# Reordering the row gathers of a fused graph-attention and routed-FFN kernel: the optional gathers and their waits

## What is computed

```python
xp = (x @ W).reshape(n, H, C)
alpha = leaky_relu(a_src[src] + a_dst[dst], 0.2)
w = exp(alpha - amax[dst]) / denom[dst]
agg = segment_sum(xp[src] * w[..., None], dst)
x = x + elu(agg.reshape(n, H * C) + bias)
weights = einsum('bsd,do->bso', layernorm(x), wr) + br      # top half is selected
y = gelu(sel @ w1 + b1) @ w2 + b2;  processed = y * w_sel
x = x + (processed + layernorm(x))
```

## Time and profile before

| | |
|---|---|
| timed runs, median of 3 | 2207.0 us |
| profiled execution: span, first to last instruction | 2573.5 us |
| profiled execution: its own time beside the span | not given |
| PE busy, share of the span | 1981.2 us, 77% |
| DVE busy | 1581.4 us, 61% |
| GpSimd busy | 1554.5 us, 60% |
| ACT busy | 744.5 us, 29% |
| mean granted TensorE clock | 0.870 of full |
| DMA | 369.12 MB, 143 GB/s |

### The profile page before, as it was taken

The page is one execution under the profiler, slowest core; times in us unless marked ns, Lnnn a source line. Parts: engine busy times, 40 slices in busy tenths (PEclk is TensorE's granted clock), DMA queues, the critical chain, the costliest instruction groups (busy, mean ns, idle before and its releaser), DMA issues.

```text
span 2573.5 us, 29095 instructions
## 1 busy us (share of the span) xinstructions
PE 1981.2 (77%) x9511; PEld 1633.8 (63%) x9512; DVE 1581.4 (61%) x3510; ACT 744.5 (29%) x1478; POOL 1554.5 (60%) x1626
## 2 busy tenths in 40 slices
PE   8935877877877877878778877877777777877787
PEld 6723666666666666666666666666666666666666
DVE  4555655665655655656656665666665665666576
ACT  4512222222322222322232232232232232223223
POOL 2366666666666666666666666666666666666630
PEclk9967988888888889889888888988988988889889
DMA  8844444444444444444444444444444444444447
GB/s 287 276 143 121 123 134 124 132 138 120 137 138 118 132 135 124 135 140 120 134 137 128 130 136 124 134 134 130 128 134 131 127 139 124 131 136 136 119 159 312
DMA packets 157137, 369.12 MB, mean 143 GB/s; under 512 B 46646, under 2 KB 73682, under 8 KB 155699
## 3 DMA queue, kind: packets, MB, share of 16 engines
q0 software_dynamic: 75088, 208.19, 30.1%
q1 hardware_dynamic: 74706, 145.62, 16.9%
q10 hardware_dynamic: 7184, 13.41, 1.4%
HBM read 328.20 MB, written 38.89 MB: 143 GB/s over the span
## 4 chain that ended last, share of the span: by engine, by line
POOL 38%; issue 23%; PE 19%; another core or an unknown queue 9%; DVE 3%; DMA 3%; ACT 2%; POOLq 1%; DVEq 0%; SPq 0%; ACTq 0%
POOL rows L692 38%; PE ag_ps L1057 7%; PE h_ps L1021 4%; PE ag_ps L934 3%; PE y_ps L1040 3%; DMA rows<-node_rows,ends 3%; POOLq L402 1%; DVE oh L1366 1%; DVE rows L1404 1%; ACT hT L808 1%; PE ag_ps L1128 0%; ACT L808 0%; PE ag_ps L1129 0%; ACT L812 0%
## 5 line engine op out<-in xcount | busy, mean ns | idle before, releaser
L692 POOL DMA_INDIRECT rows<-node_rows,ends x1563 | 1512.9, 968 | 850.6 <-issue 482.5
L1057 PE MATMUL ag_ps<-rows,oh 128*128 128x260 f32 x3518 | 845.9, 401 | 47.5 <-DVE rows L1404 34.8
L1021 PE MATMUL h_ps<-xnT,w1s 128*128 128x256 f32 x1568 | 534.0, 500 | 419.2 <-DVE zz L1385 227.1
L1057 PEld LDWEIGHTS ag_ps<-rows,oh 128*128 128x128 f32 x3518 | 716.7, 204 | 180.3 <-DVE rows L1404 37.8
L1021 PEld LDWEIGHTS h_ps<-xnT,w1s 128*128 128x128 f32 x1568 | 377.0, 250 | 517.9 <-DVE zz L1385 234.8
L1404 DVE TENSOR_TENSOR rows<-rows,xl_ps 128x512 f32<-128x512 f32 (+3 forms) x392 | 503.1, 1346 | 47.2 <-issue 26.5
L1385 DVE TENSOR_TENSOR zz<-rows,edge_dm 128x72 f32<-128x72 f32 x98 | 22.9, 233 | 695.0 <-DMA rows<-node_rows,ends 656.4
L1040 PE MATMUL y_ps<-w2s,hT 128*128 128x256 f32 x1568 | 368.0, 386 | 12.2 <-DVE oh L1366 9.2
L831 ACT COPY rows<-rows 128x780 f32<-128x780 f32 x97 | 81.6, 842 | 998.6 <-DMA rows<-node_rows,ends 998.6
L1040 PEld LDWEIGHTS y_ps<-w2s,hT 128*128 128x128 f32 x1568 | 301.7, 194 | 66.7 <-DVE oh L1366 16.6
L1366 DVE TENSOR_TENSOR oh<-xl_ps,dloc 128x2304 f32<-128x2304 f32 x98 | 249.0, 2541 | 0.0
(11 more groups left out here) (243 smaller groups left out, 1433.7 us busy)
## 6 DMA issues: line engine op xcount, KB each, us to landing
dbc<-dst SPq DMA_DIRECT2D x97, 576.0 KB
rows<-node_rows,ends POOLq DMA_INDIRECT x1563
selfr<-node_rows SPq DMA_DIRECT2D x98, 130.0 KB
base<-in_x SPq DMA_DIRECT2D x14, 896.0 KB, 7.1
base<-in_x SPq DMA_DIRECT2D x49, 256.0 KB
ffn_rows<-yb ACTq DMA_DIRECT2D x48, 256.0 KB
node_rows<-base SPq DMA_DIRECT2D x13, 910.0 KB, 5.7
base<-in_x_turned SPq DMA_DIRECT2D x14, 384.0 KB, 7.7
```

The source lines that it names most:

```text
L692: pool.indirect_dma_start(out=rows[:, b, t, :], out_offset=None, in_=table, in_offset=bass.IndirectOffsetOnAxis(ap=ends[:, b, t, 0:1], axi ...
L1021: last = nc.tensor.matmul(h_ps[:, m * PAIR:(m + 1) * PAIR], w1s[:, c, n * P:(n + 1) * P], xnT[:, c, :], start=(c == 0), stop=(c == DC - 1))
L1057: product = nc.tensor.matmul(ag_ps[b][:, 0:ROW], oh[:, b, t, :], rows[:, b, t, :], start=(t == 0), stop=False)
```

## The change

The optional gathers of a block (from the third block on) move from the end of its required ones to behind the sixth (`OPTIONAL = 5`, tile 8), with the wait for the carry, the load of the number and the two `If`s. The wait for the second layer moves to ahead of the block's first required gather, as `y_ok >= w - 5`, and the last block has it too. In the written-out form the waits for `y_ok`, `ld_ends`, `lk_ok`, `freed` and `carry_ok` are no longer made by `wait_apart` but by `pool.wait_ge` directly ahead of the gather (`held`). `optional_landed` and the table loads that stand for places of extra tiles become `value_load` with bounds.

```diff
@@ -64,7 +64,7 @@
     LOW_BITS = 8
     DIGITS, LOW_DIGITS = (32 - LOW_BITS) // 2, LOW_BITS // 2
     FREED = 6
-    LOOKED_UP, SUMMED, SECOND_LAYER = 4, (8, 11, 13), TILES - 2
+    LOOKED_UP, SUMMED, OPTIONAL = 4, (8, 11, 13), 5
     COLS = 8
     FAR = 2.0 ** 20
 
@@ -402,9 +402,12 @@
             return nc.s_assert_within(eng.value_load(win[0:1, bass.ds(COLS * w + k, 1)]), 0, most,
                                       skip_runtime_bounds_check_because="the window table holds counts and places of the edges' tiles, which lie within their number")
 
+        def counted_before(eng, w, k):
+
+            return eng.value_load(win[0:1, bass.ds(COLS * w + k, 1)], min_val=0, max_val=NW * EP // P)
+
         def optional_landed(eng, w):
-            landed = eng.value_load(win[0:1, bass.ds(COLS * w + 7, 1)])
-            return nc.s_assert_within(landed, 16, 16 * (NW + 3), skip_runtime_bounds_check_because="a parity's first node block has one gather or more, each later one two at most")
+            return eng.value_load(win[0:1, bass.ds(COLS * w + 7, 1)], min_val=16, max_val=16 * (NW + 3))
 
         def all_extra(eng):
 
@@ -418,7 +421,7 @@
             with eng.If(extras > 0):
                 n = entry(eng, w, 1, EP // P)
                 with eng.If(n > 0):
-                    before = entry(eng, w, 2, NW * EP // P)
+                    before = counted_before(eng, w, 2)
                     with eng.Fori(0, n) as j:
                         body(j, before + j)
 
@@ -431,7 +434,7 @@
             with eng.If(flag > 0):
                 with eng.Fori(0, NW) as w:
                     n = entry(eng, w, 3, EP // P)
-                    before = entry(eng, w, 4, NW * EP // P)
+                    before = counted_before(eng, w, 4)
                     with eng.If(n > 0):
                         with eng.Fori(0, n) as j:
                             body(w, j, before + j)
@@ -674,55 +677,62 @@
                 gather_row(k, m_row, m_go)
 
 
+            def held(w, semaphore, value):
+
+                if isinstance(w, int):
+                    pool.wait_ge(semaphore, value)
+                else:
+                    wait_apart(pool, (semaphore, value))
+
             def follow(w, started):
 
                 if started == LOOKED_UP:
-                    wait_apart(pool, (lk_ok, w + 1))
+                    held(w, lk_ok, w + 1)
                 for k in range(GROUPS):
                     if started == SUMMED[k]:
-                        wait_apart(pool, (freed[k], w))
-                if started == SECOND_LAYER and known(w, 5) and not (isinstance(w, int) and w == NW - 1):
-                    wait_apart(pool, (y_ok, w - 4))
+                        held(w, freed[k], w)
 
             def window(w, i, b):
-                if not known(w, 2):
-                    pool.wait_ge(ld_ends[b], 16 * (i + 1))
-
                 def gather(t, arrived):
                     pool.indirect_dma_start(out=rows[:, b, t, :], out_offset=None, in_=table,
                                             in_offset=bass.IndirectOffsetOnAxis(ap=ends[:, b, t, 0:1], axis=0)).then_inc(arrived, 16)
 
+                def optional(known_w):
+                    if known_w >= 1:
+                        held(w, carry_ok, w)
+                    if known_w < 1:
+                        pool.wait_ge(win_ld, 16)
+                    some = entry(pool, w, 5, 2)
+                    if known_w < 1:
+
+                        gather(2, gath_last[b])
+                        with pool.If(some > 0):
+                            gather(1, gath_last[b])
+                        with pool.If(some > 1):
+                            gather(0, gath_last[b])
+                    elif known_w < 2:
+
+                        gather(2, gath_last[b])
+                        with pool.If(some > 1):
+                            gather(1, gath_last[b])
+                    else:
+                        with pool.If(some > 0):
+                            gather(2, gath_last[b])
+                        with pool.If(some > 1):
+                            gather(1, gath_last[b])
+
                 for t in range(3, tiles_of(w)):
-                    if known(w, 2) and t == 3:
-                        wait_apart(pool, (ld_ends[b], 16 * (i + 1)))
+                    if t == 3:
+                        if known(w, 6):
+                            held(w, y_ok, w - 5)
+                        held(w, ld_ends[b], 16 * (i + 1))
                     if known(w, 1):
                         follow(w, t - 3)
                     gather(t, gath[b])
-                if known(w, 1):
-
-                    wait_apart(pool, (carry_ok, w))
-                    follow(w, TILES - 2)
-                if not known(w, 1):
-
-                    pool.wait_ge(win_ld, 16)
-                some = entry(pool, w, 5, 2)
-                if not known(w, 1):
-
-                    gather(2, gath_last[b])
-                    with pool.If(some > 0):
-                        gather(1, gath_last[b])
-                    with pool.If(some > 1):
-                        gather(0, gath_last[b])
-                elif not known(w, 2):
-
-                    gather(2, gath_last[b])
-                    with pool.If(some > 1):
-                        gather(1, gath_last[b])
-                else:
-                    with pool.If(some > 0):
-                        gather(2, gath_last[b])
-                    with pool.If(some > 1):
-                        gather(1, gath_last[b])
+                    if known(w, 2) and t - 3 == OPTIONAL:
+                        optional(2)
+                if not known(w, 2):
+                    optional(w)
                 if isinstance(w, int) and w == 0:
 
                     pool.wait_ge(exact_ok, 1)
```

## The result

The kernel after takes **2228.3 us** (median of 4 runs, 2227.03 to 2229.29), beside 2208.3 us for the kernel before on the same chip (2206.24 to 2211.26). The ratio is **1.0089 [1.0075, 1.0103]**: 20 us slower, where 2206 was forecast and the range ended at 2215.

What follows compares the result with a forecast made beforehand. Bound by the issue of gathers: 1563 x 1.27 = 1985 us, with 132.5 ahead and 91.1 behind, 2208.6. From the median, 2207.0 - 1 (y gate) + 0.2 (bounds) gave 2206 us, range 2186 to 2215.

Steps and rivals of the forecast that it cites:

- The cold and the warm PE: PE's loop through the y_ok gate: 20.5 us cold, after idling in a stall, 18.8 warm, against GpSimd's 20.0 us per block.
- a span near 2570 us: Profile after the change: still 3 us stalls at PE's late semaphores, since they come with the recording.
- The carry hides beside the scores: ACT's carry, 0.84 us, runs beside the scores' four steps, 1.07 us; hidden with 0.2 us to spare.
- The optional gather: Behind the sixth required gather, 7 turns (8.8 us) after the last block's; 4.8 us used, 4.0 to spare, 0 us.
- The load out of the shadow: DVE's register load before the scores: 0.63 us later with bounds in about 82 blocks, inside slack, 0 on GpSimd's path.
- the bounds' two instructions: DVE's bounded load adds two sequencer instructions, 0.19 and 0.02 us.
- The y gate: GpSimd's y_ok wait, moved to the next block's first required gather: 0.6 us more slack; -1 us, -20 as far end.
- Waits on the gathers: GpSimd's extra wait on a constant, an event of 0.02 to 0.04 us ahead of the queue, goes: 0 us.
- The bounds alone: DVE's added bound instructions, 0.21 us, count only in the last block, where nothing covers them: +0.2 us.
- The step that failed: Gathers beside DVE's turned one-hots take longer (1.48 against 0.95 us), but one such operation per block stays: 0 us.
- rival 2: Timed runs have real stalls at the y gate; 0.5 us per block goes, 2158 at the lowest; chance 0.32 faster in all.
- Rival 3: Scores 0.63 us later delay PE's sums, which the 14th required gather awaits; up to 61 us slower, 2268; chance 0.12.

Runs made afterwards that it cites:

- e4: Kernel after with DVE's table load, assertion and optional-landings wait moved ahead of its wait for the required gathers; 2208.6 us, ratio 0.9995 to the kernel before.
- e2: Kernel before, old order, with the bounded loads and every GpSimd wait made directly on the gather; 2212.7 us, ratio 1.0016 to the kernel before.
- e7: Kernel before with the bounded loads, plus two idle DVE steps ahead of the scores; 2253.7 us, ratio 1.0187 to the kernel before.
- e1: Kernel before with the bounded loads alone, one assertion per block on DVE; 2213.6 us, ratio 1.0023 to the kernel before.
- e12: Kernel after with the attention output kept in its PSUM bank, so bias and residual additions have one operand there; 2240.3 us, ratio 1.0120 to the kernel before.
- e14: Kernel after with the early table load, attention output in PSUM and one-hots given an unread accumulator; 2201.8 us, ratio 0.9951 to the kernel before.
- e10: Kernel after with the minimum in the attention output given an unread accumulator; 2236.0 us, ratio 1.0122 to the kernel before.
- e5: Kernel after with one idle DVE statistics step per block ahead of the scores; 2205.4 us, ratio 0.9976 to the kernel before.

## Why the prediction was wrong

**What bounds the kernel: right.** The stalls of the first profile are not those of timed runs, the timed kernel is bound by the issue of gathers, and 1563 gathers with their starts, a prologue and a tail give the time: 133.4 + 1521.2 + 478.1 + 93.2 = 2225.9 of a 2226.0 us span. The cold and the warm PE of the prediction are in the profile before as the granted clock: the eight matmuls that took 3.78 us after 4.08 us of idle time ran at 0.50, those that took 1.99 after 0.17 us at 1.00. The forecast that the profile after would again show a span near 2570 us was wrong; the recording didn't slow that one, nor any of the fourteen others, so it isn't a property of recording this kernel.

**The steps moved, one by one.** The carry hides beside the scores: right. The optional gather has 0.3 us of idle ahead of it like all others. The load out of the shadow: its size was right (3.4 us to the scores forecast, 3.50 measured), and so were the bounds' two instructions, 183 and 23 ns. The y gate: forecast -1 us, in the right direction; in e4 the starts are 3.8 us under e2's, and with late scores the new order is worth 22 to 25 (after against e7), though that counts the gates on the sums too. Waits on the gathers: 0 forecast, 0 measured in either order. The bounds alone: +0.2 us forecast, 4.7 measured in e1 (1.0023 [1.0013, 1.0033]); its place wasn't found, since the kernel before has no profile free of the recording's stalls to hold e1's against.

**The step that failed** is this one: "There is one such DVE operation per block before and after, so the 0.02 us per gather of the mean stay". The number of meetings stays, but not their price. A meeting costs the gathers between nothing and over half a microsecond by the moment at which the DVE operation starts in the turn, and that moment is much the same in most blocks, since DVE's work is counted from the block's last landing. Moving the scores by 0.6 to 0.7 us moved the meetings to a dearer moment: 69 of 98 one-hots start within 0.35 us in e2, 71 at 0.55 to 0.85 in after. Priced at 0, this term measured 15.6 us (after against e2), with 13 to 18 in the gathers' durations; of the 17.7 us between these two profiles some 8 are the one-hots' and some 9 the first hump's. The prediction had the size of it at hand, 0.02 us per gather being 31 us, and used it in rival 2 alone, for gathers that get faster. The step also counted one kind of meeting where there are several: the operations with two operands in SBUF had not been looked at, and they make the first hump. In the profile before, the one-hots are scattered over the turn (33 of 98 start within 0.35 us, 16 at 0.55 to 0.85), so its mean of 968 ns is an average over phases and didn't show the effect; that its stalls scatter them is likely, but wasn't tested.

**The rivals.** Rival 3 had the trigger, the scores 0.63 us later, and the sign, but not the mechanism: it wanted GpSimd to wait for the sums, and the profile has 2 us of that. Stalls of that kind came to tens of us only in the old order with late scores (e7, 26 us over free starts), where the sums stand a turn less ahead of the gates. Rival 2's gate exists, at 2.1 and 3.3 us of starts over free ones (e1 and e2, at the optional and first gathers) and not at 20, unless the scores are late.

What single operations cost shows over the same fifteen profiles (third block on, quick one-hots away): a gather that starts while the bias is added is 140 ns over 946 (393 gathers), one beside the addition of the residual 66 (627), one beside the product for the node's own row 132 (147), and with one operand of the additions in PSUM it is 0 to 2 ns over (264, e12 to e14). The runs show which operations cost and when; by what way DVE holds a gather up, none of them shows.

## What to carry to other kernels

When one engine issues a steady stream and is the bound, what another engine's operations cost it can depend on where in the turn they start. Here an edit that shifted DVE by half a turn (0.7 of 1.25 us) took the time from 2212.7 to 2228.3 us (e2 and after) with 2 us of waits. Look at the mean duration of the bounding instruction by its place, not at its mean alone, and try whether the operations beside it can be had in a form that costs nothing (here one with an operand in PSUM, or the accumulating form, 0 to 2 ns a gather for 66 to 190) before tuning the order. Treat a gain of this size from a reordering as phase until the same edit with a shifted start keeps it.

## What the runs showed that was not expected

Kernels with the same 1563 gathers and nearly the same work ran in 2201.8 to 2253.7 us, and among those whose starts are within 5 us of 476 the time still goes from 2201.8 to 2240.3 with the gathers' summed durations, 1493 to 1527 us (e10 had 1531 at 2236.0). A slower instruction made the kernel faster: 170 us more on DVE, 13.9 us less in all. So did idle work: e5 does 98 operations more than the kernel after and takes 23 us less (25 by the ratios). And a profile can mislead by its own stalls: one execution of the kernel before was recorded at 2573.5 us for 2207, while the fifteen profiles since have spans 1.8 to 2.2 us under their own time.
